# Image and text attention on one core: the scores of every second head as three rounded products of high and low parts

## What is computed

```
h = concat([patches(x) @ w_tok.T + b_tok, txt], axis=1)      # (32, 273, 128)
q, k, v = split(layernorm(h) @ w_qkv.T + b_qkv)              # 8 heads of 16
q, k = rope2d(q), rope2d(k)
logits = einsum('bhid,bhjd->bhij', q, k) * scale
logits = einsum('bhij,gh->bgij', logits, w_pre)              # heads mixed before the softmax
attn = einsum('bhij,gh->bgij', softmax(logits), w_post)      # and after it
h = h + (attn @ v) @ w_out.T + b_out
h = h + experts(layernorm(h))                                # top 2 of 8, then a layer norm
```

## Time and profile before

| | |
|---|---|
| median of 3 runs | 1436.22 us |
| the profiled execution, its own time | 1437.18 us |
| its span, first to last instruction | 1435.3 us |
| busy: TensorE (matmuls), weight loads | 1317.1 us (92%), 1099.1 us (77%) |
| busy: ScalarE, VectorE, GpSimd | 1024.7, 894.0, 837.9 us |
| mean granted TensorE clock | 0.968 |

### The profile page before, as it was taken

One profiled execution on the slowest core, in us unless ns is written; L12 is line 12 of the kernel. 1 busy time (PEld: TensorE's weight loads), 2 busy tenths in 40 slices (PEclk: granted clock), 3 DMA queues, 4 the chain that ended last, 5 costly groups with the idle time before them and its releaser, 6 DMA issues.

```text
span 1435.3 us, 34511 instructions
## 1 busy us (share of the span) xinstructions
PE 1317.1 (92%) x8386; PEld 1099.1 (77%) x8387; DVE 894.0 (62%) x3124; ACT 1024.7 (71%) x3008; POOL 837.9 (58%) x1845
## 2 busy tenths in 40 slices
PE   5899999999999999999999999997699999997874
PEld 4777788777887777787778877776599999996331
DVE  3776666776666766667666667664355444443777
ACT  2688887888888888878888888887155555553676
POOL 2136665566665566655666655666556666665444
PEclk9999999999999999999999999999599999998987
DMA  6001111111110101110111101100222222222763
GB/s 238 19 28 32 37 51 35 31 35 31 50 38 31 35 31 34 50 35 31 35 31 50 38 31 35 31 15 28 72 70 78 77 77 77 75 73 61 198 178 95
DMA packets 69507, 82.39 MB, mean 57 GB/s; under 512 B 11650, under 2 KB 59773, under 8 KB 68946
## 3 DMA queue, kind: packets, MB, share of 16 engines
q1 hardware_dynamic: 57264, 57.17, 13.6%
q0 software_dynamic: 11328, 19.07, 4.3%
q10 hardware_dynamic: 866, 5.60, 0.9%
HBM read 52.13 MB, written 30.65 MB: 58 GB/s over the span
## 4 chain that ended last, share of the span: by engine, by line
PE 55%; DVE 18%; POOL 10%; issue 9%; ACT 5%; DMA 1%; DVEq 1%; ACTq 0%; POOLq 0%; SPq 0%
PE PS L1285 10%; PE PS L1438 10%; PE PS L1247 8%; PE PS L1201 6%; PE PS L1265 4%; DVE bst L876 4%; DVE nmax L954 3%; PE PS L1425 3%; PE PS L1427 3%; PE PS L1426 3%; PE PS L1291 2%; POOL rs L466 2%; ACT E L696 2%; DVE xn L901 2%; POOL qT L489 2%
## 5 line engine op out<-in xcount | busy, mean ns | idle before, releaser
L1247 PE MATMUL PS<-kT,qs 128*128 128x273 f32 x1024 | 281.8, 398 | 1.8 <-ACT E L696 1.4
L1285 PE MATMUL PS<-AT,VP 128*128 128x273 f32 x1024 | 279.4, 395 | 0.0
L696 ACT ACTIVATE E<-PS,nmax 128x273 f32<-128x273 f32 x512 | 243.9, 484 | 25.7 <-DVE nmax L954 21.1
L954 DVE TENSOR_REDUCE nmax<-PS 128x2 f32<-128x546 f32 (+1 forms) x288 | 206.8, 718 | 72.3 <-PE PS L1247 72.3
L585 POOL DMA_INDIRECT dram_routed<-xr,slu x192 | 189.0, 984 | 60.5 <-issue 60.5
L1247 PEld LDWEIGHTS PS<-kT,qs 128*128 128x128 f32 x1024 | 184.4, 190 | 36.2 <-issue 2.9
L641 POOL DMA_INDIRECT dram_results<-arena,du x152 | 166.0, 1092 | 62.9 <-issue 53.3
L723 ACT COPY AT<-PS 128x512 f32<-128x512 f32 x256 | 150.1, 586 | 60.7 <-PE PS L1265 60.7
L1285 PEld LDWEIGHTS PS<-AT,VP 128*128 128x128 f32 x1024 | 175.5, 191 | 20.6
L1265 PEld LDWEIGHTS PS<-small,E 128*128 128x128 f32 x1024 | 126.2, 141 | 53.1 <-ACT ATR L730 22.0
L1265 PE MATMUL PS<-small,E 128*128 128x128 f32 x1024 | 156.4, 274 | 8.9 <-ACT ATR L730 8.7
(11 more groups left out here) (191 smaller groups left out, 2790.4 us busy)
## 6 DMA issues: line engine op xcount, KB each, us to landing
arena<-in_x SPq DMA_DIRECT2D x32, 588.0 KB
arena<-dram_routed SPq DMA_DIRECT2D x76, 144.0 KB
dram_h<-H SPq DMA_DIRECT2D x32, 147.0 KB
w1hl<-dram_h SPq DMA_DIRECT2D x32, 147.0 KB
stage<-dram_results SPq DMA_DIRECT2D x16, 196.0 KB
AT<-dram_results SPq DMA_DIRECT2D x16, 196.0 KB
out<-VP SPq DMA_DIRECT2D x32, 98.0 KB
dram_routed<-xr,slu POOLq DMA_INDIRECT x192, 2.3
```

The costliest lines, as they stand in the source:

```text
L696: nc.scalar.activation(bank, PS[0:rows, 2 * ((par + u) % 2) + t, 0:N], ACT.Exp, bias=nmax[0:rows, u, t:t + 1], accum_out=esum[0:rows, u, t ...
L954: v.tensor_reduce(nmax[0:rows, u], PS[0:rows, b0:b0 + 2, 0:N], AX.X, ALU.max, negate=True).then_inc(S["max"], 1)
L1247: last = mm(PS[0:rows, 2 * ((par + u) % 2) + t, 0:N], q, kT[:, par, 0:N], start=True, stop=True)
L1285: last = mm(acc, VP[:, par, g, c, :], AT[:, g, c, :], start=(g == 0 and c == 0), stop=False)
```

## The change

Heads 0, 2, 4 and 6 (steps 1, 3, 5, 7) get their scores from three rounded products, heads 1, 3, 5 and 7 keep the plain product.

- `q_hi` on ScalarE writes the scaled queries of even heads into `qhi`, of type fp32r, with a ring of two; those of odd heads into `qs`, now a ring of two.
- `q_lo` on VectorE is new: it forms the scaled queries again and subtracts the rounded ones (`qlo`). It stands two steps ahead of its `scores`: after `head_max` in steps 8, 1, 3 and 5.
- `k_hi` on ScalarE is new, once an image: it copies kT, rounded, into `khi`, after the exponentials of step 8.
- `k_lo` on VectorE is new, once an image: kT minus `khi` (`klo`), after `head_max` in step 0.
- `scores` of an even head is six matmuls over 274 columns in place of two (of two records each) over 273.
- `khi`, `klo`, `qhi` and `qlo` lie in the tile `rounded`.

```diff
+        khi, klo = (rounded_[:, i * 2 * NP:(i + 1) * 2 * NP].rearrange("p (u n) -> p u n", u=2) for i in range(2))
+        qhi, qlo = (rounded_[:, 4 * NP + i * 2 * MQ:4 * NP + (i + 1) * 2 * MQ].rearrange("p (u n) -> p u n", u=2)
+                    for i in range(2))
...
                         pool.wait_ge(S["q_scaled"], NH * (b - 1))
+                        pool.wait_ge(S["q_lo"], NH // 2 * (b - 1))
                         pool.wait_ge(S["qr"], b - 1)
...
-                nc.scalar.activation(qs[:, g % QR, :], qT[:, par, 0:MQ], ACT.Copy, scale=wpre[:, g:g + 1]
+                dst = (qhi, qs)[g % 2][:, g // 2 % 2, :]
+                nc.scalar.activation(dst, qT[:, par, 0:MQ], ACT.Copy, scale=wpre[:, g:g + 1]
                                      ).then_inc(S["q_scaled"], 1)
+
+            def k_hi(b, par):
+                act.wait_ge(S["qk_sb"], 2 * b + 2)
+                if not below(b, 2):
+                    act.wait_ge(S["scores_ps"], NU * (b - 1))
+                nc.scalar.copy(khi[:, par], kT[:, par]).then_inc(S["k_hi"], 1)
...
             normedT(0)
+            k_hi(0, 0)
             q_hi(0, 0, 0)
...
+                    if u == 8 and has["emb"]:
+                        k_hi(i + 1, 1 - par)
...
+            def q_lo(i, par, g):
+
+                dve.wait_ge(S["q_scaled"], NH * i + g + 1)
+                dve.wait_ge(S["qk_sb"], 2 * i + 1)
+                v.scalar_tensor_tensor(qlo[:, g // 2 % 2, :], qT[:, par, 0:MQ], wpre[:, g:g + 1],
+                                       qhi[:, g // 2 % 2, :].bitcast(f32), ALU.mult, ALU.subtract
+                                       ).then_inc(S["q_lo"], 1)
+
+            def k_lo(b, par):
+                dve.wait_ge(S["k_hi"], b + 1)
+                v.tensor_tensor(klo[:, par], kT[:, par], khi[:, par].bitcast(f32), ALU.subtract).then_inc(S["k_lo"], 1)
...
+            q_lo(0, 0, 0)
...
+                    if u == 0 and has["attn"]:
+                        k_lo(i, par)
+                    lead = ahead_of(i, u, 2, has)
+                    if lead and lead[1] % 2 == 1:
+                        q_lo(lead[0], par if u + 2 < NU else 1 - par, lead[1] - 1)
...
                 else:
-                    pe.wait_ge(S["q_scaled"], NH * i + u)
+                    pe.wait_ge(S["q_lo"], NH // 2 * i + u // 2 + 1)
+                    if u == 1:
+                        pe.wait_ge(S["k_lo"], i + 1)
...
+                    else:
+                        o, hi, lo = PS[:, bank + t, 0:NV], qhi[:, ring, cols], qlo[:, ring, cols]
+                        mm(o, hi, khi[:, par, 0:NV], start=True, stop=False)
+                        mm(o, hi, klo[:, par, 0:NV], start=False, stop=False)
+                        last = mm(o, lo, khi[:, par, 0:NV], start=False, stop=True)
                 last.then_inc(S["scores_ps"], 1)
```

More of the change, by code:

```diff
@@ L152, in early_fusion_kernel @@
         QR = 4
-        qs = sb("qs", [D, QR, MQ])
+        qs = sb("qs", [D, 2, MQ])
+        khi, klo = (rounded_[:, i * 2 * NP:(i + 1) * 2 * NP].rearrange("p (u n) -> p u n", u=2) for i in range(2))
+        qhi, qlo = (rounded_[:, 4 * NP + i * 2 * MQ:4 * NP + (i + 1) * 2 * MQ].rearrange("p (u n) -> p u n", u=2)
+                    for i in range(2))
         qrf = sb("qrf", [D, NH, RT])
@@ L249, in early_fusion_kernel @@
             tok_ps xnT_ps qk_ps v_ps h0 bn1 bn2 bn3 stats1 stats2 stats3 rstd1 rstd1_steps xn xnT_sb hb rope qk_sb
-            q_scaled qr vp scores_ps max exp recip probs probs_act own probsT_ps probsT_sb av_ps attn_sb proj_ps h1
+            q_scaled k_hi k_lo q_lo qr vp scores_ps max exp recip probs probs_act own probsT_ps probsT_sb av_ps attn_sb proj_ps h1
             rstd2 kept_norm rstd2_steps y2 xhat x2T_ps x2T_sb gate_ps gate_sb top8 logit_gap gap_exp choice_steps masks both
@@ L1237, in scores @@
                     pe.wait_ge(S["qk_sb"], 2 * i + 2)
-                else:
-                    pe.wait_ge(S["q_scaled"], NH * i + u)
+                elif u % 2 == 0:
+                    pe.wait_ge(S["q_scaled"], NH * i + u)
+                else:
+                    pe.wait_ge(S["q_lo"], NH // 2 * i + u // 2 + 1)
+                    if u == 1:
+                        pe.wait_ge(S["k_lo"], i + 1)
                 if not (below(i, 1) and u < 2):
                     pe.wait_ge(S["exp"], 2 * (NU * i + u - 1))
+                bank, ring = 2 * ((par + u) % 2), (u - 1) // 2 % 2
                 for t in range(2):
+                    cols = slice(t * 128, (t + 1) * 128)
                     if u == 0:
-                        rows, q = RM, qrf[:].rearrange("p g n -> p (g n)")[:, t * RM:(t + 1) * RM]
-                    else:
-                        rows, q = 128, qs[:, (u - 1) % QR, t * 128:(t + 1) * 128]
-                    last = mm(PS[0:rows, 2 * ((par + u) % 2) + t, 0:N], q, kT[:, par, 0:N], start=True, stop=True)
+                        q = qrf[:].rearrange("p g n -> p (g n)")[:, t * RM:(t + 1) * RM]
+                        last = mm(PS[0:RM, bank + t, 0:N], q, kT[:, par, 0:N], start=True, stop=True)
+                    elif u % 2 == 0:
+                        last = mm(PS[:, bank + t, 0:N], qs[:, ring, cols], kT[:, par, 0:N], start=True, stop=True)
+                    else:
+                        o, hi, lo = PS[:, bank + t, 0:NV], qhi[:, ring, cols], qlo[:, ring, cols]
+                        mm(o, hi, khi[:, par, 0:NV], start=True, stop=False)
+                        mm(o, hi, klo[:, par, 0:NV], start=False, stop=False)
+                        last = mm(o, lo, khi[:, par, 0:NV], start=False, stop=True)
                 last.then_inc(S["scores_ps"], 1)
```

## The result

The changed kernel takes **1466.98 us** (median of 4 runs, 1465.87 to 1469.45), the kernel before on the same chip 1435.68 (1434.65 to 1436.59): 1.0218 times the time, 95% interval 1.0203 to 1.0233, or 31.3 us more. Forecast were 1457 us, between 1447 and 1477. The sign and the range held; a third of the increase was not in my sum.

What follows compares the result with a forecast made beforehand. The chain was taken as 16.1 us per image on TensorE, then 14.3 on VectorE, GpSimd and ScalarE in series. −0.38 + 0.83 + 0.22 = +0.67 us over thirty images, +20.6 with the start, gave 1457 us, range 1447 to 1477.

Steps and rivals of the forecast that it cites:

- q_lo of steps 3 and 5: VectorE, behind the maxima, ahead of token_stats and residual: 0.41 us each, +0.83 us per image, delaying everything behind.
- q_lo of steps 8 and 1, k_hi, no cost: VectorE subtractions and ScalarE's rounded copy fall in idle time: nothing per image; the copy +0.5 us once before the loop.
- the cover of 0.60: VectorE's gap of 0.60 us in front of VP in step 8, said to hide the subtraction there.
- the wait for k_lo: TensorE ahead of the scores of step 1: waits of 0.39 and 0.04 us, on average +0.22 us per image.
- Two heads of TensorE's stretch: Split heads of steps 1 and 3, in TensorE's part of the chain: 0.19 us gained each, −0.38 us per image.
- gl at 1.2 us: Sign: TensorE's wait for the logits copy grows from 0.8 to about 1.2 us, staying off the chain.
- ATR: Sign: TensorE's wait for this copy, ahead of the transposes of step 8, grows from 0.25 to about 1.1 us.
- The period: Sign: one image of the attention loop takes 31.0 us, against 30.34 before.
- TensorE as the bound: Rival: other engines have slack, all four heads' gains count, 24 us faster, 1412 us; chance 0.10.
- the clock: Rival: longer waits lower TensorE's clock in one image in ten, +48 us, 1505; chance 0.03 shared with dear products.
- the hold-up: Rival: GpSimd and VectorE contend, k_lo and step 8's q_lo grow by up to 0.585 us, 1472 us; chance 0.08.

Runs made afterwards that it cites:

- two operations alone: Kernel before plus two unused subtractions shaped like q_lo on VectorE in steps 3 and 5, nobody waiting for them: 1459.47 us, 1.0168 times before.
- k_lo first: Changed kernel with k_lo ahead of the maximum of step 0 instead of behind it: 1461.04 us, 1.0186 times the kernel before.
- the run of the zeros: Changed kernel without any q_lo or k_lo, low parts being zeros written once, all six matmuls still running: 1435.44 us, 0.9999 times before.

## Why the prediction was right, and where its sum was not

**q_lo of steps 3 and 5: right.** +0.83 us was the term, and the stretch grew by 0.83; the operation's 475 ns against 484, its 0.39 to 0.40 us in the row against 0.41. The two operations alone gave 24.0 us, 0.80 for each of 30 images (their long stretch grew by 0.75 and 0.77; where the last 0.07 of the 0.83 comes from stays open).

**q_lo of steps 8 and 1, k_hi, no cost: right for themselves.** One operation in step 8 measured as nothing, and k_hi too. GpSimd holds q_lo up by 0.12 us, inside the cover of 0.60. What I had not followed is what the meeting does to GpSimd: by the later HB the maximum of step 0 comes 0.12 us later in every second image (4.09 us behind the transposes of step 8 instead of 3.97), and k_lo with it. That cost stands in the wait for k_lo below; it was not measured by itself.

**Two heads of TensorE's stretch: mis-sized.** I took −0.19 each, the middle between a pitch that goes by columns and one that doesn't. The head of step 3 gave −0.14 and that of step 1 −0.05: the pitch is 0.128 us, not 0.126, and the first matmul behind a wait takes 0.23 to the next. Where the same head waits for nothing (k_lo first, an image clear of a jump) it takes 0.76 us. The term is −0.19, not −0.38.

**The wait for k_lo: mis-sized.** I had +0.22 as the mean of 0.39 and 0.04, with 0.1 us from VectorE's end to the first matmul. That way is 0.24 us long, and in the image clear of a jump k_lo comes 0.12 us later besides:

```profile
620.00 0.67 DVE L965 TENSOR_SCALAR E<-E,rsum 128x256 f32<-128x256 f32 x1
620.59 0.71 DVE L980 TENSOR_REDUCE nmax<-PS 68x2 f32<-68x546 f32 x1
621.23 0.45 DVE L954 TENSOR_TENSOR rounded<-kT,rounded 128x294 fp32r<-128x294 f32 x1
```

The waits are 0.50 and 0.31, so the term is +0.40, not +0.22. My remark that the first weights aren't loaded ahead any more was the right worry with the wrong price.

**The jump back: in the sum without its name.** At the jump TensorE's stretch is 16.40 us, 0.33 more than before; clear of it 16.06, 0.07 more. Of the 0.26 between them, 0.19 is the longer wait for k_lo. My pair of 0.39 and 0.04 had that already, since VectorE's maximum is late at the jump in the kernel before too (4.31 us behind the transposes, 3.97 an image later). New is ScalarE's late copy. From the weighted products ahead of the rest transposes to the second of these, TensorE takes 1.27 us at the jump and 1.15 clear of it, before 1.23 and 1.15: 0.04 us more in every second image, 0.02 on average. In this kernel the wait for k_lo stands ahead of that point; with k_lo first, TensorE waits 0.43 us there.

Together 0.83 − 0.19 + 0.40 + 0.02 = +1.06 per image against a forecast of +0.67; measured are +1.01 to +1.03. The heads and the wait for k_lo, 0.19 and 0.18 us off in the same direction, are the third of the increase that my sum lacked.

**The range.** It held, but not for its reason. Its upper end had room for a k_lo held up by 0.585 us, which did not happen. With the other high ends alone (0.48 twice, −0.33) and my 0.22 for k_lo, the sum is +0.85 per image and 1462 us, below the 1467 measured. The bounds of the heads and of the way from VectorE to the first matmul were too narrow.

**The signs.** gl at 1.2 us: as forecast. ATR: 0.85 instead of 1.1. I had added the whole delay to the wait for ATR, but TensorE spends part of it at gl, 0.4 us of it; with the two operations alone, where no head is cheaper, the wait for ATR likewise grew from 0.3 to 0.6 only. The period: 31.36 instead of 31.0. The rivals: TensorE as the bound fell with the run of the zeros: all four heads are cheaper, nothing is added to VectorE, and the long stretch still takes 14.31 and 14.32 us, so the heads of steps 5 and 7 give nothing; the clock stayed at 1.00 in all 29 windows of 31.35 us between 100 and 1009 us of the changed kernel, and the waits of 1.2 us did not lower it; the hold-up came to a fifth of its price on q_lo and not at all on k_lo (0.445 to 0.452 us in all 32 images), and the long one fell on GpSimd's sl.

None of the versions is measurably faster than the kernel before. Heads 1 and 2 split would gain 0.15 us of 30.30 per image if every image went as those clear of a jump do; a loop that keeps them and loads no code was not tried.

## What to carry to other kernels

Before making one engine's work cheaper, find the stretches in which that engine is last, and count the gain only there; here an operation of 0.48 us on an engine with a third of its time idle cost 0.40 us in the row that the other stretch ends on, and nothing in a gap of 0.6 us elsewhere. Ask also which engine is the next to be last: two heads cheaper by 0.30 us gave 0.18. Time the way from a producer's end to the first matmul behind a wait as its own term. And after adding instructions to a loop, look at the queue that loads instructions over one turn: here it moved where it had been silent, the jump was dearer in the same versions, and four images in a turn made it worse.

## What the runs showed of the hardware that I had not expected

- A rounded matmul over 274 columns comes every 0.128 us, over 256 columns every 0.118; the first one behind a wait for its operands starts 0.24 us after VectorE's end and takes 0.23 to the second.
- A loop of two images ran without loading instructions; 8 to 16 more matmul records in it came with 5 packets per turn, and ScalarE 0.44 to 0.57 us late behind the jump instead of 0.08. That the loading is the cause is not shown.
- With four images in a turn of the kernel before, the jump cost VectorE 2.86 and 1.09 us without work, and after TensorE had idled 2.7 us its granted clock was 0.59 and 0.56, near the 1.2 GHz level, for four us. In the changed kernel, with a wait of 1.2 us per image, it stayed at 1.00.
- VectorE and GpSimd slow each other at a meeting, GpSimd more: q_lo 0.59 instead of 0.475, VectorE's scaling 0.67 instead of 0.49; msb 0.41 instead of 0.23, tv 0.34 instead of 0.19, and sl 1.09 instead of 0.28 beside k_lo.
